# One gate product in a single reduced-precision pass, and three steps moved, in an attention and expert-routing kernel

## The reference, cut to what matters

```python
x = layernorm(x)
q, k, v = x @ Wq + bq, x @ Wk + bk, x @ Wv + bv          # 512 x 512 each
gate  = sigmoid(silu(x @ Wg1 + bg1) @ Wg2 + bg2)          # Wg1: 512 x 16, Wg2: 16 x 512
alpha = 0.9 * gate + 0.1                                  # decay of the state, per token and channel
intra = softmax(mask(q @ k.T / sqrt(32))) @ v             # inside a chunk, 16 heads of 32
S     = alpha_t * S + k_t v_t                             # the running state; inter = q_t @ S
x     = x + inter + intra
x     = x + shared_ffn(layernorm(x)) + routed_ffn(layernorm(x))
```

## Time and profile before

| | |
|---|---|
| median of 3 runs | 4699.62 us (4697.8 to 4702.13) |
| the profiled execution | 4707.31 us |
| its span, first to last instruction | 4705.4 us |
| busy: PE / DVE / ACT / POOL | 95% / 75% / 48% / 28% of the span |
| mean granted TensorE clock | 0.982 |
| first phase | from the start to about 3770 us |

### The profile page before, as it was taken

The page is one execution under the profiler, slowest core; times in us unless marked ns, Lnnn a source line. Parts: engine busy times, 40 slices in busy tenths (PEclk is TensorE's granted clock), DMA queues, the critical chain, the costliest instruction groups (busy, mean ns, idle before and its releaser), DMA issues. The chain is left out here.

```text
span 4705.4 us, 183217 instructions
## 1 busy us (share of the span) xinstructions
PE 4477.3 (95%) x74416; PEld 3897.4 (83%) x74416; DVE 3518.8 (75%) x7639; ACT 2271.9 (48%) x7475; POOL 1334.0 (28%) x1275
## 2 busy tenths in 40 slices
PE   6999999999999999999999999999999969999998
PEld 5888888888888888888888888888888859999998
DVE  5777777777777777777777777777777768888887
ACT  4444444444444444444444444444444436666665
POOL 2111111111111111111112121211111146666666
PEclk9999999999999999999999999999999979999999
DMA  2000000101000000000000000001000069999997
GB/s 66 31 31 31 31 31 31 36 31 36 28 34 31 31 31 31 31 31 31 31 31 31 31 31 31 31 31 35 31 31 31 31 207 268 270 268 265 267 271 193
DMA packets 195054, 358.52 MB, mean 76 GB/s; under 512 B 16736, under 2 KB 92896, under 8 KB 194352
## 3 DMA queue, kind: packets, MB, share of 16 engines
q1 hardware_dynamic: 160848, 269.47, 16.9%
q0 software_dynamic: 33632, 79.73, 7.8%
HBM read 243.87 MB, written 107.50 MB: 75 GB/s over the span
## 5 line engine op out<-in xcount | busy, mean ns | idle before, releaser
L589 ACT ACTIVATE PR<-PR,MX 128x64 f32<-128x64 f32 x2048 | 682.6, 335 | 811.6 <-DVE MX L1171 811.6
L475 POOL TENSOR_TENSOR RI<-PV,AL 128x512 f32<-128x512 f32 x65 | 78.5, 1208 | 2540.0 <-DVE PV L1125 2540.0
L727 PE MATMUL bank<-XTh,wsguh 128*128 128x256 f32 x1536 | 447.0, 291 | 0.0
L1663 PE MATMUL ebank<-XH,WH 128*128 128x256 f32 x1536 | 431.2, 281 | 6.8 <-DVE XL L1745 6.8
L728 PE MATMUL bank<-XTl,wsguh 128*128 128x256 f32 x1536 | 430.4, 280 | 0.0
L729 PE MATMUL bank<-XTh,wsgul 128*128 128x256 f32 x1536 | 430.4, 280 | 0.0
L1663 PE MATMUL ebank<-XH,WL 128*128 128x256 f32 x1536 | 429.7, 280 | 0.0
L1663 PE MATMUL ebank<-XL,WH 128*128 128x256 f32 x1536 | 429.5, 280 | 0.0
L589 ACT ACTIVATION_READ_ACCUMULATOR PR<-PR,MX 128x1 f32 x2048 | 383.0, 187 | 0.0
L1738 DVE TENSOR_TENSOR WL<-WS,WH 128x768 fp32r<-128x768 f32 (+1 forms) x455 | 370.5, 838 | 16.2
L1600 ACT ACTIVATE WH<-WS 128x768 fp32r<-128x768 f32 (+1 forms) x455 | 325.3, 747 | 26.3 <-DMA WS<-in_L_ffn_w_down_dram 26.3
(11 more groups left out here) (228 smaller groups left out, 13456.6 us busy)
## 6 DMA issues: line engine op xcount, KB each, us to landing
WS<-in_L_ffn_w_gate_dram SPq DMA_DIRECT2D x65, 768.0 KB
WS<-in_L_ffn_w_up_dram SPq DMA_DIRECT2D x65, 768.0 KB
WS<-in_L_ffn_w_down_dram SPq DMA_DIRECT2D x65, 768.0 KB
norm_rows<-XR SPq DMA_DIRECT2D x64, 576.0 KB, 3.1
X<-in_L_attn_x_dram SPq DMA_DIRECT2D x66, 512.0 KB, 3.6
out_dram<-X SPq DMA_DIRECT2D x64, 512.0 KB, 2.9
CR<-token_counts,count_at POOLq DMA_INDIRECT x136
XG<-norm_rows,row_at POOLq DMA_INDIRECT x132, 6.4
```

The source lines that it names most:

```text
L475: nc.gpsimd.tensor_tensor(inverse[:, :, 0:half], PV[:, :, :], running[:, :, HC:half:-1], ALU.mult).then_inc(folded.sem, 1)
L589: ins = nc.scalar.activation(PR[b][:, j, :], PR[b][:, j, :], ACT.Exp, bias=MX[b][:, j:j + 1], scale=1.0, accum_out=SU[b][:, j:j + 1])
L727: nc.tensor.matmul(out, sh, mh, start=first, stop=False)
L1663: last = nc.tensor.matmul(bank[HID[m]][:, a * CAP:(a + 1) * CAP], w, x[odd][:, c, :], start=(c == 0 and i == 0), stop=(c == KC - 1 and i = ...
```

## The change

**Stacked copies.** `Wg1` is loaded three times, into columns 0 to 15, 32 to 47 and 64 to 79 of `wg1_f`, and the bias likewise, so that the hidden values come out three times, on partitions 0, 32 and 64 and up. `wg2` becomes float32r with three copies on the same partitions: the high part twice, and from partition 64 the low rest. The moving operand is a new tile `sg`, float32r: its high part is made by ACT (`s1_high`), and partitions 32 to 63 are overwritten by the low rest by DVE (`s1_low`). One pass then adds the three products.

**Orders.** On PE the key product's half 0 goes in front of gate2, and outputs 0 comes after half 1. On ACT gate1 n goes in front of exp 0. On DVE silu1 n goes in front of softmax_b 0.

```diff
-BANK_OF = {"G1": 3, "Qa": 0, "G2a": 2, "G2b": 3, "Ka": 0, "Qb": 1, ...
+BANK_OF = {"G1": 3, "Qa": 0, "Ka": 0, "G2a": 2, "G2b": 3, "Qb": 1, ...
@@ SP, set-up
-        WEIGHT_DMAS = 8
+        WEIGHT_DMAS = 5 + 3 * len(COPIES)                 # COPIES = (0, 32, 64)
-            sp.dma_start(wg1_f[:, :, 0:GH], Wg1.rearrange("(c p) n -> p c n", p=P)).then_inc(weights_in, 16)
-            sp.dma_start(wg2[0:GH, :], Wg2).then_inc(weights_in, 16)
+            for at in COPIES:
+                sp.dma_start(wg1_f[:, :, at:at + GH], Wg1.rearrange("(c p) n -> p c n", p=P)).then_inc(weights_in, 16)
+                sp.dma_start(wg2_f[at:at + GH, :], Wg2).then_inc(weights_in, 16)
+                sp.dma_start(b1[at:at + GH, :], bg1.rearrange("(p o) -> p o", o=1)).then_inc(weights_in, 16)
@@ ACT
+            def s1_high(t):
+                act.wait_ge(s1_made.sem, t.value(s1_made))
+                act.wait_ge(g2_filled.sem, t.value(g2_filled, back=1))
+                nc.scalar.activation(sg[:, :], s1[:, :], ACT.Copy).then_inc(s1h_ready.sem, 1)
...
+            nc.scalar.activation(wg2[:, :], wg2_f, ACT.Copy).then_inc(rw_ready, 1)
...
+                    gate1(n)
                     exp(t, 0)
-                    gate1(n)
                     q_evac(n, 0)
+                    s1_high(n)
                     gate2(n, 0)
@@ PE
-                    ... wg2[:, m * P:(m + 1) * P], s1[:, :], start=True, stop=True)
+                    ... wg2[:, m * P:(m + 1) * P], sg[:, :], start=True, stop=True)
...
                     scores(t, 1)
+                    project(t, 0, wk, k_filled, ("Ka", "Kb"), parts=(0,))
                     gate2(t, 0)
                     gate2(t, 1)
                     turn_probs(t, 0)
-                    project(t, 0, wk, k_filled, ("Ka", "Kb"), parts=(0,))
+                    project(t, 0, wk, k_filled, ("Ka", "Kb"), parts=(1,))
                     outputs(t, 0)
-                    project(t, 0, wk, k_filled, ("Ka", "Kb"), parts=(1,))
                     scores(t, 2)
@@ DVE
-                dve.wait_ge(g2_filled.sem, t.value(g2_filled, back=1))
+                dve.wait_ge(s1h_ready.sem, t.value(s1h_ready, back=1))
...
+            def s1_low(t):
+                dve.wait_ge(s1h_ready.sem, t.value(s1h_ready))
+                v.tensor_tensor(sg[32:64, :], s1[32:64, :], sg[32:64, :].bitcast(f32), ALU.subtract).then_inc(s1_ready.sem, 1)
...
+            v.tensor_tensor(wg2[64:96, :], wg2_f[64:96, :], wg2[64:96, :].bitcast(f32), ALU.subtract).then_inc(w_low, 1)
...
+                    silu1(n)
                     softmax_b(t, 0)
-                    silu1(n)
+                    s1_low(n)
                     softmax_a(t, 1)
```

More of the change, by code:

```diff
@@ L33 @@
 GH = 16
+COPIES = (0, 32, 64)
 GP = 128
@@ L62 @@
           + [slice(2 * WPART + i * DIM, 2 * WPART + (i + 1) * DIM) for i in range(FC)])
-BANK_OF = {"G1": 3, "Qa": 0, "G2a": 2, "G2b": 3, "Ka": 0, "Qb": 1, "Kb": 2, "ATr0": 3, "V0": 0, "V1": 1, "ATr1": 2,
+BANK_OF = {"G1": 3, "Qa": 0, "Ka": 0, "G2a": 2, "G2b": 3, "Qb": 1, "Kb": 2, "ATr0": 3, "V0": 0, "V1": 1, "ATr1": 2,
            "X2Ta": 3, "X2Tb": 0, "KTok0": 2, "RL": 1, "KTok1": 3, "GU0": 2, "RLT": 1, "GU1": 0, "GU2": 3, "DK": 1,
@@ L143, in phase_tokens @@
         wg1 = [sb(f"wg1{i}", [P, KC, GP], f32r) for i in "hl"]
-        wg2 = sb("wg2", [GP, DIM])
+        wg2 = sb("wg2", [GP, DIM], f32r)
         rwT = sb("rwT", [P, KC, 2 * E], f32r)
@@ L167, in phase_tokens @@
         s1 = sb("s1", [GP, TB])
+        sg = sb("sg", [GP, TB], f32r)
         AL = sb("AL", [P, KC, NS * PAD])
@@ L253, in phase_tokens @@
         g1_tanh = event("g1_tanh", 2)
+        s1_made = event("s1_made")
+        s1h_ready = event("s1h_ready")
         s1_ready = event("s1_ready")
@@ L344, in phase_tokens @@
                 staged.append((st, high, low, rows[:, :, i * TB:(i + 1) * TB]))
+        wg2_f = OTs[0][:, :, :].rearrange("p a b -> p (a b)")
         wg1_f = XR[:, 1, 0:KC * GP].rearrange("p (c n) -> p c n", c=KC)
@@ L417, in _ @@
             nc.gpsimd.memset(wg1_f, 0.0)
-            nc.gpsimd.memset(wg2[:, :], 0.0)
+            nc.gpsimd.memset(wg2_f, 0.0)
             nc.gpsimd.memset(b1[:, :], 0.0).then_inc(gate_clear, 1)
@@ L641, in _ @@
             nc.scalar.mul(bq4s[:, :], bq4[:, :], SCALE).then_inc(rw_ready, 1)
-            act.wait_ge(rw_ready, 4)
+            act.wait_ge(rw_ready, 5)
             def q_evac(t, k):
@@ L649, in k_evac @@
                 qk_evac(t, k, k_filled, k_ready, KT, bk4, 1.0, ("Ka", "Kb"))
-            act.wait_ge(w_low, len(staged) + 1)
+            act.wait_ge(w_low, len(staged) + 2)
             t = Turn(0, 0)
@@ L655, in _ @@
             gate1(t)
+            s1_high(t)
             q_evac(t, 0)
@@ L759, in gate2 @@
                     m = 2 * k + a
-                    last = nc.tensor.matmul(b[:, a * TB:(a + 1) * TB], wg2[:, m * P:(m + 1) * P], s1[:, :], start=True, stop=True)
+                    last = nc.tensor.matmul(b[:, a * TB:(a + 1) * TB], wg2[:, m * P:(m + 1) * P], sg[:, :], start=True, stop=True)
                 last.then_inc(g2_filled.sem, 1)
@@ L977, in _ @@
             last.then_inc(rw_turned, 1)
-            pe.wait_ge(rw_ready, 4)
-            pe.wait_ge(w_low, len(staged) + 1)
+            pe.wait_ge(rw_ready, 5)
+            pe.wait_ge(w_low, len(staged) + 2)
             first = Turn(0, 0)
@@ L1103, in silu1 @@
                 dve.wait_ge(g1_tanh.sem, t.value(g1_tanh))
-                dve.wait_ge(g2_filled.sem, t.value(g2_filled, back=1))
+                dve.wait_ge(s1h_ready.sem, t.value(s1h_ready, back=1))
                 dve.wait_ge(qd_ready.sem, t.value(qd_ready, back=1))
                 link(v.memset(running[:, :, 0:1], 0.0))
-                v.scalar_tensor_tensor(s1[:, :], t1[:, :], 1.0, z1[:, :], ALU.add, ALU.mult).then_inc(s1_ready.sem, 1)
+                v.scalar_tensor_tensor(s1[:, :], t1[:, :], 1.0, z1[:, :], ALU.add, ALU.mult).then_inc(s1_made.sem, 1)
+            def s1_low(t):
+                dve.wait_ge(s1h_ready.sem, t.value(s1h_ready))
+                v.tensor_tensor(sg[32:64, :], s1[32:64, :], sg[32:64, :].bitcast(f32), ALU.subtract).then_inc(s1_ready.sem, 1)
             def decays(t):
@@ L1304, in _ @@
                             rwT[:, :, 0:E].bitcast(f32), ALU.subtract).then_inc(w_low, 1)
-            dve.wait_ge(w_low, len(staged) + 1)
+            dve.wait_ge(rw_ready, 2)
+            v.tensor_tensor(wg2[64:96, :], wg2_f[64:96, :], wg2[64:96, :].bitcast(f32), ALU.subtract).then_inc(w_low, 1)
+            dve.wait_ge(w_low, len(staged) + 2)
             t = Turn(0, 0)
@@ L1310, in _ @@
             silu1(t)
+            s1_low(t)
             decays(t)
```

1 line of the change is left out of this document (removed).

## The result

The changed kernel takes 4742.84 us (median of 4 runs, 4740.39 to 4748.83) against 4700.82 (4 runs, 4697.8 to 4702.13) on the same chip: ratio 1.0092, 95% interval 1.0075 to 1.011, 42 us slower. The profiled execution before, 4707.31 us, lies 6.5 above its median of 4700.82, the changed one 1.0 above its own, so some 5.5 of the 42 us are outside these accounts. The granted clock is 0.976 on average (before 0.982).

The account below looks back on a forecast made before the run. PE is 95% busy, but its list and the ACT/DVE chain end almost together at outputs 1. Loop +25.6 and set-up +4.3 make +29.9 on the 4699.6 median: 4729.5 us; own range 4712 to 4745 (70%), wider 4698 to 4775.

Parts of the forecast that it names:

- The chain in front of outputs 1: ACT and DVE work through weights 1, which outputs 1 waits for; claimed to decide, outputs 1 later by 0.54 us.
- PE's own list: Rival: PE's instruction sequence decides the time, gaining 1.33 + 0.2 us a turn, 98 us in all: 4606; chance 4%.
- the term for the later gate: Loop, outputs 1 delayed by the half key product before gate2: 0.54, 0.45, 0.54, 0.07 us a pass, +25.6 us.
- a clock at 0.50 elsewhere than at the loop edges: Sign against the forecast: PE's granted clock at the 1.2 GHz level anywhere but the loop edges would show it wrong.
- Gate2 as one pass: On PE, gate2's four matmuls: 1.80 us in float32, 0.47 as float32r, saving 1.33 us a turn.
- Softmax_b 0, softmax_a 1: On DVE, softmax_b 0 moves later by 0.82 us and softmax_a 1 from 2106.32 to 2107.00, behind s1_low.
- weights 0's slack: On DVE, 0.49 us of idle time in front of weights 0, which moves by 0.3 us at most.
- The later Tanhs: On ACT, gate2's first half arrives 0.91 us later, moving its Tanhs and exp 1 by as much.
- From there on: Behind exp 1: softmax_b 1 later by 0.66 us (0.25 hidden by scans), outputs 1 by 0.54 (0.12 to spare).
- The set-up: Before the loop: six more weight DMAs and wg2's subtraction, less gate2's saving, delay the start: +4.3 us.
- The clock: Rival: idle PE before outputs 1 drops the clock, 1.8 us a fall; 4772 in half of 48 turns, 4816 in all; 15%.
- The instruction supply: Rival within the forecast's own range: PE's smaller "issue" waits within turns shrink by at most 0.8 us a pass, −13 us.

Follow-up runs that it names:

- the fill: Changed kernel plus six query-product passes computed once more per turn behind turn_probs 1, to fill PE's wait before outputs 1; 4751.66 us, 1.0105 to the kernel before.

## Why the prediction was right in direction and short in size

The chain in front of outputs 1 decides, not PE's own list: right. The prediction's sum was 29.9 us and the profile shows 36.3 (by the medians 42). That the two are so near is in part luck: the term for the later gate was twice too large (25.6 for 12.8), and stalls and falls of the clock that the sum didn't hold made up for it with 20.8. By one of the prediction's own signs, a clock at 0.50 elsewhere than at the loop edges, it was wrong. Step by step:

- *Gate2 as one pass.* 1.33 us saved on PE: right (0.47 for four). That all of it is lost again is shown by the pass alone, 0.2% slower.
- *Softmax_b 0, softmax_a 1.* Moves of 0.82 and 0.68 were predicted; softmax_b 0 moved by 0.79 and softmax_a 1 by 0.72, and weights 0's slack hid it, as said. `s1_low` takes 0.42 and is 0.45 from the next start, the upper bound and not the 0.36 taken.
- *The later Tanhs: the term that was mis-sized.* +0.91 predicted, +0.73 measured. The key half starts at 7.35 and not at 7.47, since PE follows the evacuation by 0.05 and not by the 0.15 that I carried over from another pair of engines' rows. Then the four Tanhs take 1.57 us in a row instead of 1.70: before, the second pair had waited for gate2's second half (the third Tanh starts 0.49 behind the second, the others 0.37 apart; now all are 0.36 to 0.37 apart), and the faster pass has taken that wait away. I had read 1.70 as ACT's work. So exp 1 moves by 0.60 instead of 0.91.
- *From there on* the steps held: softmax_b 1 at +0.42 and outputs 1 at +0.28, so 0.18 and 0.14 are absorbed on the way, where 0.25 and 0.12 had been predicted. Turn 3 shows +0.18 for +0.45, turn 1 +0.06 for +0.07. The term of 25.6 us measures 12.8.
- *The set-up.* 2.3 for 4.3. Six more DMAs moved the last by 2.2 us, just below the lower bound of 2.5. By the 50 ns of dispatch on GpSimd's path from the Trainium skill ("DMA: Bandwidth & Descriptors", "Anatomy of one DMA — SWDGE (gpsimd) path") it would be an estimated 0.3; the trace of SP's queue, with its 2.2, disagrees.
- *The clock.* Counted as a rival with 15% and left out of the sum; it came in part. I had priced it for half or all of 48 turns; it came in 14 of them and three times more in turn 1, at 0.7 to 1.1 us and not 1.8. That is 17.9 us, which together with 12.8 and 2.7 leaves 2.9 of the 36.3 without a place. The Trainium skill, "TensorE: Matmul & The Clock Gate", "HAM oscillation — how this bites in real kernels", describes the loss as paid in every iteration that waits, for a kernel with longer waits than here (some 3 to 5 us); here turns with the same wait differ, with a fall in 5 of 16 turns 3 behind a wait of 1.4 us.
- *The instruction supply.* Predicted to shrink by at most 0.8 us a pass; it grew. "Issue" waits in line 856 went from 31.8 us in 15 waits (line 842 before) to 49.9 in 42. This is the step of the argument that failed: the move of outputs 0 behind key half 1 was given no cost at all. It takes away the 12 long passes between two groups of small matmuls. Outputs 0 and scores 2 are then 160 records of small matmuls in a row, and at certain places among them PE is out of instructions. In turn 2 this stall is mostly paid from the idle time ahead of outputs 1, so its price isn't its length but the fall that follows it.

**What is shown and what is open.** Shown: the orders on PE carry the whole loss, and putting outputs 0 alone back takes away those stalls, the falls of both kinds in turns 2 and 3 and 20.8 of 33.6 us. The falls of the first kind go with the wait in front of outputs 1, but this is less firm. Over turns 2 to 4 without a stall in scores 2, waits of some 1.4 us were followed by a fall in 9 of 24 turns of the changed kernel, in 18 of 31 with the orders alone and in only 1 of 19 without the orders on ACT and DVE; waits of 0.74 us or less in the fill in none of 33, and waits of 0.45 to 1.16 us with the orders alone (turn 3) in none of 16. In the changed kernel, the fill and the kernel without orders on ACT and DVE, all 31 falls of the second kind lie in turns with a stall in scores 2. Only some stalled turns have a fall (5 of 23, 11 of 14, 15 of 28 in those three), more often those with a long stall: 16 of the 20 with 1.1 us or more, 15 of the 45 with less. In turn 1, where the stall comes just behind scores 2, the one fall behind it lies in each of the three kernels in the turn with the longest stall (1.43, 1.48 and 1.40 us). Open: what else decides over a fall, whether the stall or the small matmuls around it count for more, and why PE runs out of instructions at these places; no run separates them.

## What to carry to other kernels

Before a product is moved ahead of the one that a chain waits for, count what the chain pays. Here half a key product in front of gate2 cost 12.8 us, while the version that leaves gate2 in front and makes the extra operations mostly in idle time of ACT and DVE is 0.3% faster than the kernel before. When moving a block of PE work, also look at what it had kept apart: here, twelve long passes between two groups of small matmuls kept PE from running out of instructions and kept its idle time in small pieces. And try the parts of a change together as well as one by one: the same pass cost 10 us in the old orders and saved 70 in the new ones. A row that merges several instructions may contain a wait; read its length as work only if the releaser of each is known.

## What the runs showed of the hardware

- Behind a wait of PE of 1.4 us, with small matmuls after it, the granted clock went from full speed to 0.50 in some turns (9 of 24, 18 of 31 and 1 of 19 in three kernels), for 3.4 us each time; in the fill, with waits of 0.74 us or less, none of that kind was seen in 33 turns.
- PE stood still for up to 1.5 us among 160 records of small matmuls in a row without waiting for any engine, always at the same place of its loop.
- A subtraction of 32x256 takes 0.42 us on DVE, as long as 128x256 does; on GpSimd 1.17.
